# Query projection, range check and bias rows moved among the later spare jobs of a one-core attention kernel, and 29 instead of 30 key tiles on VectorE

## The chip, the core and the metric

One core of one Trainium2 chip runs the whole computation. Its engines work side by side and each takes its own instructions in order: TensorE (PE, matmuls into PSUM; PEld are its weight loads), VectorE (DVE), ScalarE (ACT), GpSimd (POOL), and SyncE (SP), which only issues DMAs here. The metric is the device time of one execution in microseconds (us).

## The reference, cut to what matters

Cross attention of 1024 queries over 6404 keys with 16 heads of width 8, followed by a feed-forward part with a main branch and two of eight experts, chosen once for all tokens.

```python
q = layernorm(x) @ Wq + bq;  k = ctx @ Wk + bk;  v = ctx @ Wv + bv      # 16 heads of 8
attn = softmax(clip(q @ k.T * 8 ** -0.5, -10000, 10000))                # nan: 1 / keys
x = x + (attn @ v) @ Wo + bo
main = gelu(h @ W1m + b1m) @ W2m + b2m                                  # h = layernorm(x)
x = x + a * main + (1 - a) * experts(h)                                 # a = clip(alpha, .1, 1)
```

The softmax is computed without a maximum when a bound on all scores shows that this is safe. That bound is what the code calls the check of ranges.

## The kernel before

**Passes, steps, tiles.** There are eight passes: four groups of four heads times two halves of 512 queries. In a pass each of 51 key tiles (50 of 128 keys, one tail of 4) is a step. A step has four chunks, one for each head, of 128 keys x 512 queries; the tail step has one chunk for all heads. Three chunks make a *tile* of 1536 columns in PSUM (`ps`, two of them), for which ScalarE runs one exponential (line 540) into one of four buffers. There are 496 tiles (`NT`), numbered through all passes. TensorE computes the scores of tile t+2 (line 1222), does what spare job stands at tile t, waits for exponential t and adds to the output the steps of values whose last chunk lies in tile t (line 1315). As four tiles hold three steps, every fourth tile has no step of values. TensorE is thus two tiles of scores ahead of ScalarE.

**Key tiles on VectorE.** `D_PLAN` takes 30 of the 400 full key tiles from ScalarE: VectorE computes their exponentials by a polynomial (lines 932 to 973, about 19 us of VectorE a key tile). A row of the plan is: pass, key tile, the tiles at which TensorE computes the four heads' scores into the spare bank, the order of the heads, and the tile at which the values are used. Such a score matmul runs beside those of the tile, on other rows of the array.

**Spare jobs.** `SPARE` lists what TensorE writes to the spare PSUM bank (`po[1]` in pass 0), by tile: V's projection in chunks (`V_AT`: chunk 2 at tile 2, then every third tile to chunk 12 at tile 32), the two halves of the range bound (`BOUND_TILES`, 3 and 7), the gather of their maxima (10), the rows (12: bo, alpha and the experts' first biases spread over the partitions), the scores for VectorE, and at a pass's end the tokens (line 1268). There is one bank: TensorE's `spare_job` (line 1232) waits until VectorE's `take_job` (line 737) has released the job before (`spare_taken`). Behind V's chunks 2 to 7, VectorE also splits K's segments 4 to 9 into two parts, which SyncE stores to DRAM and loads back in the layout of the scores.

**The head.** Ahead of the first scores TensorE transposes the context in 13 pieces and projects each to K (line 1097), ScalarE reads both. In between stand q replicated for group 0 (`qrep`, line 1131) and q itself (`qT`, line 1137, read by ScalarE in line 526). VectorE picks the two parts of group 0's q (`pick_q`, lines 680 to 682); its second half is picked behind bound 0. q itself serves the range check (`q_abs`, line 726) and groups 1 to 3: `split_q` (lines 672, 674, behind bound 1, tile 7) writes two parts, which GpSimd stores to DRAM (line 478) and loads back (line 382, twelve loads) and then fills V's tail buffer (lines 482, 485). VectorE waits for those fills before it copies V's tail in (line 897).

**The flag.** The gather's result is a flag (line 757). `NPRE` is 14: all engines run tiles 0 to 13, then wait for the flag and branch: the fast branch goes on with the tiles, the other computes everything in a general way. The inputs here take the fast branch.

**The epilogue.** `EPI_AT` puts steps of the first half's output projection, second layernorm and first feed-forward layer among the tiles of the last pass. Step 1 is the residual (line 776).

Of the kernel before, what the change touches and what calls it, by code (L numbers as in the profile page):

```python
# [33 lines left out]
BANK = 512  # L34
KCH = -(-NK // BANK)
NHALF = NQ // BANK
# [20 lines left out]
NPRE = 14  # L57
V_AT = {c: 3 * c - 4 for c in range(2, VCH)}
BOUND_TILES, GSUM_TILE, ROWS_TILE = (3, 7), 10, 12
# [59 lines left out]
]  # L119
DKT = [[kt for p, kt, *_ in D_PLAN if p == q] for q in range(NP)]  # L120

# [1373 lines left out]
```

## Time and profile before

| | |
|---|---|
| median of 3 runs | 776.45 us (776.31 to 778.46) |
| the profiled execution | 778.63 us, of which the span is 776.8 |
| PE busy | 729.8 us, 94% |
| ACT busy | 717.9 us, 92% |
| DVE busy | 618.7 us, 80% |
| POOL busy | 28.1 us, 4% |
| the exponentials, line 540 | 496 in 708.1 us |
| steps of values, line 1315, VectorE's and ScalarE's | 3200 matmuls |
| chain that ended last | PE 66%, ACT 17%, issue 14%, DVE 2%, DMA 1% |

Busy times are of one profiled execution. Matmuls are pipelined: several records overlap, so the time from one group's start to the next one's start is what a group costs, not its length. A row of the timeline gives the start, the length of a merged group, the engine, the line, what is written from what, how many instructions, and in brackets how long the engine was idle before it and what released it.

### The profile page before, as it was taken

Reading aid. Unit: us, or ns where it says so; the run is one execution under the profiler, and the core shown is the slowest. Engines: PE = TensorE matmul, PEld = TensorE weight load, DVE = VectorE, ACT = ScalarE, POOL = GpSimd, SP = SyncE. Lnnn points to the kernel's source line nnn. Section 1 sums busy time; section 2 is a strip of 40 time slices with the busy share of each in tenths; the row PEclk is TensorE's granted clock in tenths of the full one; section 3 lists DMA queues with packets and bytes.
Section 4 is the critical chain, followed back from the end, with each engine's and each line's share of the span. In section 5 each row is a group of like instructions: output and inputs, shape, how many; then the busy total and the mean of one; then the engine's idle time right before and its main releaser. Section 6 shows DMA issues by size and latency. Waiting matters only on the chain.

```text
span 776.8 us, 13354 instructions
## 1 busy us (share of the span) xinstructions
PE 729.8 (94%) x5398; PEld 218.1 (28%) x5398; DVE 618.7 (80%) x857; ACT 717.9 (92%) x575; POOL 28.1 (4%) x49
## 2 busy tenths in 40 slices
PE   5999999999999999999999999999999999999898
PEld 3534322222222222222222222222222223222457
DVE  6873369799969998799889998999889976986320
ACT  3788999999999999999999999999999999999751
POOL 5204000000000000000000000000000000000000
PEclk9899999999999999999999999999999999999999
DMA  5669100111110000111100000111100000000011
GB/s 166 179 196 258 42 1 2 35 35 35 35 35 1 2 1 1 37 41 43 42 10 2 1 1 18 35 35 40 47 1 1 1 1 1 2 0 2 1 54 30
DMA packets 18043, 28.53 MB, mean 37 GB/s; under 512 B 5286, under 2 KB 8732, under 8 KB 17980
## 3 DMA queue, kind: packets, MB, share of 16 engines
q1 hardware_dynamic: 12730, 23.71, 10.4%
q0 software_dynamic: 4032, 3.30, 1.8%
q8 instruction: 45, 0.74, 0.4%
q10 hardware_dynamic: 1218, 0.64, 0.3%
q14 instruction: 18, 0.15, 0.1%
HBM read 19.50 MB, written 8.13 MB: 36 GB/s over the span
## 4 chain that ended last, share of the span: by engine, by line
PE 66%; ACT 17%; issue 14%; DVE 2%; DMA 1%; SPq 0%; ACTq 0%
PE po L1315 34%; PE ps L1222 19%; ACT region_ctx L540 12%; ACT probs_own L540 4%; PE ps L1328 2%; PE po L1108 2%; PE po L1338 1%; PE ps L1097 1%; PE po L1301 1%; PE po L1222 1%; DVE pT L657 1%; DMA xres<-in_x 1%; PE po L1199 1%; PE ps L1085 1%; PE po L1169 0%
## 5 line engine op out<-in xcount | busy, mean ns | idle before, releaser
L540 ACT ACTIVATE region_ctx<-ps 128x1536 f32<-128x1536 f32 x372 | 523.0, 1493 | 9.8 <-PE ps L1222 8.6
L1315 PE MATMUL po<-region_ctx,v 128*9 128x512 f32 x2220 | 386.0, 595 | 0.3 <-ACT region_ctx L540 0.3
L1222 PE MATMUL ps<-qst,region_k 32*128 32x512 f32 x1480 | 249.1, 492 | 31.7 <-ACT region_ctx L540 22.5
L1222 PEld LDWEIGHTS ps<-qst,region_k 32*128 32x128 f32 x1480 | 95.7, 181 | 400.4 <-ACT region_ctx L540 279.7
L1315 PE MATMUL po<-probs_own,v 128*9 128x512 f32 x740 | 191.0, 595 | 0.0
L540 ACT ACTIVATE probs_own<-ps 128x1536 f32<-128x1536 f32 x124 | 185.1, 1493 | 2.3 <-PE ps L1222 2.2
L932 DVE TENSOR_SCALAR region_kT<-po 128x512 f32<-128x512 f32 x120 | 82.4, 687 | 44.0 <-PE po L1222 43.3
L935 DVE SCALAR_TENSOR_TENSOR region_kT<-region_kT,po 128x512 f32<-128x512 f32 x120 | 81.7, 681 | 0.3
L973 DVE SCALAR_TENSOR_TENSOR dres<-region_kT,dres 128x1024 f32<-128x1024 f32 x60 | 73.5, 1225 | 1.9
L970 DVE SCALAR_TENSOR_TENSOR dres<-region_kT,dres 128x1024 f32<-128x1024 f32 x60 | 73.2, 1220 | 0.2
L964 DVE SCALAR_TENSOR_TENSOR region_kT<-region_kT 128x1024 f32<-128x1024 f32 x60 | 73.1, 1219 | 0.0
L962 DVE SCALAR_TENSOR_TENSOR dres<-region_kT 128x1024 f32<-128x1024 f32 x60 | 73.1, 1218 | 0.0
L967 DVE SCALAR_TENSOR_TENSOR dres<-dres,region_kT 128x1024 f32<-128x1024 f32 x60 | 73.0, 1216 | 0.0
L1315 PEld LDWEIGHTS po<-region_ctx,v 128*9 128x9 f32 x2220 | 41.8, 88 | 66.7 <-issue 62.0
L1222 PE MATMUL po<-qst,region_k 32*128 32x512 f32 x120 | 55.4, 462 | 0.4 <-DVE xres L776 0.4
L953 DVE TENSOR_SCALAR region_kT<-region_kT 128x1024 uint32<-128x1024 uint32 x60 | 41.0, 684 | 0.0
L1315 PE MATMUL po<-dres,vd 128*9 128x512 f32 x240 | 31.4, 595 | 0.0
L697 DVE COPY v<-po 128x512 f32<-128x512 f32 (+1 forms) x13 | 8.8, 680 | 24.5 <-PE po L1108 24.5
L1315 PEld LDWEIGHTS po<-probs_own,v 128*9 128x9 f32 x740 | 19.5, 88 | 26.7 <-issue 25.6
L492 POOL TENSOR_TENSOR rstd<-rstd,powers 128x4 f32<-128x4 f32 x1 | 1.1, 1082 | 590.2 <-DVE rstd L629 590.2
L1222 PEld LDWEIGHTS po<-qst,region_k 32*128 32x128 f32 x120 | 21.8, 182 | 1.0 <-issue 1.0
L914 DVE COPY region_kT<-po 128x512 f32<-128x512 f32 x7 | 4.8, 692 | 17.0 <-PE po L1301 17.0
(219 smaller groups left out, 354.1 us busy)
## 6 DMA issues: line engine op xcount, KB each, us to landing
region_k<-k_dram SPq DMA_DIRECT2D x40, 320.0 KB, 3.3
k_dram<-kparts SPq DMA_DIRECT2D x18, 320.0 KB, 3.8
qst<-q_dram POOLq DMA_DIRECT2D x12, 128.0 KB, 9.6
region_ctx<-in_ctx SPq DMA_DIRECT2D x2, 624.0 KB, 9.0
q_dram<-dres POOLq DMA_DIRECT2D x2, 512.0 KB, 4.1
k_dram<-kparts SPq DMA_DIRECT2D x2, 322.0 KB, 8.4
region_ctx<-in_ctx SPq DMA_DIRECT2D x1, 576.0 KB, 7.4
xres<-in_x SPq DMA_DIRECT2D x1, 512.0 KB, 4.4
```

Source lines behind the costliest of these rows:

```text
L540: act.activation(probs_of(t)[:, 0:cols], ps[t % NSB][:, 0:cols], ACT.Exp, scale=ESCALE).then_inc(exp_ready, 1)
L932: d_count(("u", c), v.tensor_scalar(du[:, i % 2, part], src, MAGIC, None, ALU.add))
L935: v.scalar_tensor_tensor(df[:, i % 2, part], du[:, i % 2, part], MAGIC, src, ALU.subtract, ALU.subtract).then_inc(spare_taken, 1)
L953: d_count(("e", i), v.tensor_scalar(u.bitcast(U32), u.bitcast(U32), 23, None, ALU.logical_shift_left))
L962: d_count(("q1", i), v.scalar_tensor_tensor(res, f, A1, f, ALU.add, ALU.mult))
L964: d_count(("q2", i), v.scalar_tensor_tensor(q, f, A2, f, ALU.add, ALU.mult))
L967: d_count(("p1", i), v.scalar_tensor_tensor(res, res, B1, u, ALU.add, ALU.mult))
L970: d_count(("p2", i), v.scalar_tensor_tensor(res, q, B2, res, ALU.add, ALU.mult))
L973: v.scalar_tensor_tensor(res, f, R0, res, ALU.subtract, ALU.mult).then_inc(d_ready, 1)
L1108: last = mm(dst[:, (t % 4) * P:(t % 4 + 1) * P], lhsT, wv_sb[:, :], start=True, stop=True)
L1222: return mm(dst, kst[r, kt * P:(kt + 1) * P], qst[r, g, queries], start=True, stop=True)
L1315: last = mm(dst[QUAD * j:QUAD * j + V9, :], w, src, start=first, stop=last_one, skip_group_check=True)
```

## The change

q itself is no longer projected in the head. It becomes two spare jobs, at tiles 33 and 35, behind V's last chunk; VectorE instead of ScalarE reads it, and in the same job makes the absolute values for the bound. Behind its second half VectorE splits q and finishes the sum that the flag needs. The bounds move from tiles 3 and 7 to 37 and 39, the gather from 10 to 41, the rows from 12 to 44. The second half of the picked q moves from behind bound 0 to behind V's chunk 2. The branch moves from tile 14 to tile 47, so that all V chunks lie ahead of it; the keys' tail and the residual's bias are handled by VectorE behind the branch, the bias behind the wait for GpSimd's fills.

The plan of VectorE's key tiles has 29 rows. Pass 0 has none any more (it had one), pass 2 has five instead of four, pass 4 four instead of five, and all tiles are set anew; the first score job stands at 50 instead of 38. That makes 1492 chunks and 498 tiles, the last of one chunk. The epilogue's steps move too, and the tokens of pass 6 from tile 436 to 440.

```diff
-NPRE = 14
+NPRE = 47
 V_AT = {c: 3 * c - 4 for c in range(2, VCH)}
-BOUND_TILES, GSUM_TILE, ROWS_TILE = (3, 7), 10, 12
+Q_TILES, BOUND_TILES, GSUM_TILE, ROWS_TILE = (33, 35), (37, 39), 41, 44
 D_PLAN = [
-    (0, 49, (38, 40, 43, 45), (3, 1, 2, 0), 60),
-    (1, 49, (49, 52, 56, 59), (0, 1, 2, 3), 75),
-    (1, 48, (62, 71, 74, 76), (3, 1, 2, 0), 91),
+    (1, 49, (50, 52, 55, 57), (3, 1, 2, 0), 75),
+    (1, 48, (61, 64, 73, 75), (0, 1, 3, 2), 87),
...
-    (7, 47, (445, 448, 455, 458), (0, 1, 2, 3), 476),
-    (7, 46, (461, 466, 469, 475), (0, 3, 1, 2), 484),
+    (7, 47, (445, 447, 454, 456), (0, 2, 3, 1), 472),
+    (7, 46, (461, 467, 470, 473), (0, 2, 3, 1), 496),
 ]
-EPI_AT = [440, 444, 452, 464, 472, 480, 488]
+EPI_AT = [444, 452, 464, 476, 484, 488, 492]
...
-            act.wait_ge(bqs_ready, 1)
-            for n in range(NHALF):
-                act.wait_ge(q_psum, n + 1)
-                act.activation(qT[:, n * BANK:(n + 1) * BANK], po[n][:, :], ACT.Identity, bias=bqs[:, 0:1], scale=QSCALE,
-                               accum_out=ksum[:, KCH + n:KCH + n + 1]).then_inc(q_ready, 1)
...
-            link(v.scalar_tensor_tensor(q_abs, qT[:, :], -1.0, qT[:, :], ALU.mult, ALU.max))
...
                 if kind == "v":
                     take_v(i, src).then_inc(spare_taken, 1)
+                    if i == 2:
+                        pick_q(1)
+                elif kind == "q":
+                    cols = slice(i * BANK, (i + 1) * BANK)
+                    step(v.tensor_scalar(qT[:, cols], src[:, :], QSCALE, bqs[:, 0:1], ALU.mult, ALU.add))
+                    v.scalar_tensor_tensor(q_abs[:, cols], qT[:, cols], -1.0, qT[:, cols], ALU.mult, ALU.max).then_inc(spare_taken, 1)
+                    step(v.tensor_reduce(ksum[:, KCH + i:KCH + i + 1], qT[:, cols], AX.X, ALU.add))
+                    if i == NHALF - 1:
+                        split_q()
+                        step(v.tensor_reduce(kcol[:, 3:4], ksum[:, :], AX.X, ALU.add))
+                        step(v.tensor_tensor(kcol[:, 5:6], kcol[:, 3:4], bkc[:, :], ALU.add))
+                        v.tensor_scalar(kcol[:, 4:5], kcol[:, 5:6], 0.0, None, ALU.mult).then_inc(bounds_ready, 1)
                 elif kind == "bound":
                     v.tensor_reduce(gcol[:, i:i + 1], src[0:2 * H, :], AX.X, ALU.max).then_inc(spare_taken, 1)
-                    if i == 0:
-                        pick_q(1)
-                    else:
-                        split_q()
...
             with dve.If(safe != 0):
                 flink = chain(fast_step)
-                for n in range(JOBS_PRE, JOBS_V):
-                    take_job(n, flink)
-                    if SPARE[n][1:] == ("v", VCH - 4):
-                        add_bo(flink)
-                    if SPARE[n][1:] == ("v", VCH - 2):
-                        take_last_keys()
+                take_last_keys()
                 dve.wait_ge(spare_taken, JOBS_V)
                 dve.wait_ge(vones_ready, 2 + GH)
                 for j in range(GH):
                     r = slice(QUAD * j, QUAD * (j + 1))
                     v.tensor_copy(vtail[r, :, QUAD * j:QUAD * j + D],
                                   v9[r, FULL, :, 0:D].rearrange("p (g j) d -> p g j d", g=NG)[:, :, j, :]).then_inc(vtail_ready, 1)
+                add_bo(flink)
...
-            for n in range(NHALF):
-                pe.wait_ge(qrep_ready, n + 1)
-                mm(po[n][:, :], wq_sb[:, :], xnT[:, n * BANK:(n + 1) * BANK], start=True, stop=True).then_inc(q_psum, 1)
...
+                elif kind == "q":
+                    last = mm(po[1][:, :], wq_sb[:, :], xnT[:, i * BANK:(i + 1) * BANK], start=True, stop=True)
```

## Rows read from the trace of the kernel before

**Rows 1.** Busy by stretch: PE, PEld, DVE, ACT, POOL; clock, DMA share, GB/s.

```profile
24.50:37.00 12.50, 12.50 (x53) 6.66 (x52) 9.73 (x17) 10.97 (x31) 0.00 (x0) 1.00 0.54 157
98.00:600.00 502.00, 474.56 (x3664) 115.89 (x3660) 454.69 (x550) 498.14 (x368) 0.00 (x0) 1.00 0.08 21
```

**Rows 2.** Timeline of ACT: exponentials of tiles 0, 45 to 47, and 48.

```profile
37.05 1.45 ACT L540 ACTIVATE probs_own<-ps 128x1536 f32<-128x1536 f32 x1
...
106.21 4.21 ACT L540 ACTIVATE region_ctx<-ps 128x1536 f32<-128x1536 f32 x3
110.20 1.56 ACT L540 ACTIVATE probs_own<-ps 128x1536 f32<-128x1536 f32 x1
```

**Rows 3.** Chain that ended last, 20 to 45 us: start, length, what.

```profile
25.13 1.72 PE po L1137 x4
...
42.02 1.09 PE po L1108 x8
43.11 0.97 PE po L1315 x8
```

**Rows 4.** Exponentials by stretch: tiles 0-32, 50-65, passes 3, 4, 7; length, busy.

```profile
37.00:89.95 52.95, 46.44 (x33) 1.00 0.68 193
...
112.86:135.48 22.62, 21.82 (x17) 1.00 0.00 1
...
302.83:387.71 84.88, 84.08 (x63) 1.00 0.13 36
387.72:470.00 82.28, 81.57 (x61) 1.00 0.02 5
...
639.60:725.43 85.83, 84.17 (x62) 1.00 0.00 1
```

**Rows 5.** Timeline of PE: bound 0, gather, and rows, between the scores around them.

```profile
44.02 0.50 PE L1222 MATMUL ps<-qst,region_k 32*128 32x512 f32 x3
...
44.45 0.62 PE L1253 MATMUL po<-xn,bounds 128*32 128x512 f32 x1
...
46.28 0.73 PE L1222 MATMUL ps<-qst,region_k 32*128 32x512 f32 x6
...
56.04 0.21 PE L1257 MATMUL po<-ident,gcol 32*1 32x32 f32 x2
...
59.68 0.50 PE L1222 MATMUL ps<-qst,region_k 32*128 32x512 f32 x3
...
60.63 0.50 PE L1222 MATMUL ps<-qst,region_k 32*128 32x512 f32 x3
```

**Rows 6.** Timeline of DVE: absolute values, bound's maximum, and the split of q.

```profile
40.63 1.23 DVE L726 SCALAR_TENSOR_TENSOR xn<-qT 128x1024 f32<-128x1024 f32 x1
...
45.53 0.68 DVE L745 TENSOR_REDUCE gcol<-po 32x1 f32<-32x512 f32 x1 [0.43 <-PE po L1253]
...
52.54 0.67 DVE L672 CAST dres<-qT 128x1024 fp32r<-128x1024 f32 x1
...
53.25 1.23 DVE L674 TENSOR_TENSOR dres<-qT,dres 128x1024 fp32r<-128x1024 f32 x1
```

**Rows 7.** Timeline of DVE: its copy of V's last chunk (tile 32).

```profile
92.22 0.56 DVE L697 COPY v<-po 128x384 f32<-128x384 f32 x1 [3.73 <-PE po L1108]
```

**Rows 8.** Timeline of POOL's loads and fills, and of a copy beside a fill.

```profile
11.65 5.61 DVE L657 COPY pT<-ident 128x64 f32<-128x64 f32 x2
11.66 5.52 POOL L466 MEMSET region_ctxT<- 1x6432 f32 x1 [7.32 <-DVE xn L634]
...
59.96 6.99 POOL L382 DMA_DIRECT2D qst<-q_dram  x12 [4.30 <-DMA q_dram<-dres]
...
67.55 0.56 POOL L485 MEMSET vtail<- 4x4 f32 x4
```

**Rows 9.** Timeline: score job behind the residual, and the exponential it delayed.

```profile
657.07 0.47 PE L1222 MATMUL po<-qst,region_k 32*128 32x512 f32 x1 [0.45 <-DVE xres L776]
...
659.00 1.46 ACT L540 ACTIVATE probs_own<-ps 128x1536 f32<-128x1536 f32 x1 [0.78 <-PE ps L1222]
```

More of the change, by code:

```diff
@@ L153 @@
                + [(NORM_AT[p], "tokens", p) for p in range(NP - 1)] + [(t, "v", c) for c, t in V_AT.items()]
-               + [(t, "bound", n) for n, t in enumerate(BOUND_TILES)]
+               + [(t, "q", n) for n, t in enumerate(Q_TILES)] + [(t, "bound", n) for n, t in enumerate(BOUND_TILES)]
                + [(GSUM_TILE, "gsum", 0), (ROWS_TILE, "rows", 0)])
 JOBS_PRE = sum(t < NPRE for t, _, _ in SPARE)
-JOBS_V = SPARE.index((V_AT[VCH - 1], "v", VCH - 1)) + 1
+JOBS_V = JOBS_PRE
 SPLIT_BEHIND = {SPARE.index((V_AT[c], "v", c)): s for c, s in zip(range(2, VCH), range(4, NSEG))}
@@ L318, in build @@
         var_ready, std_ready, xn_ready = sem("var_ready"), sem("std_ready"), sem("xn_ready")
-        xnT_psum, xnT_ready, q_psum, q_ready = sem("xnT_psum"), sem("xnT_ready"), sem("q_psum"), sem("q_ready")
+        xnT_psum, xnT_ready = sem("xnT_psum"), sem("xnT_ready")
         ctxT_psum, ctxT_ready, tailT_ready = sem("ctxT_psum"), sem("ctxT_ready"), sem("tailT_ready")
@@ L669, in split_q @@
             def split_q():
-                dve.wait_ge(q_ready, NHALF)
                 v.tensor_copy(qparts[:, 0, :], qT[:, :]).then_inc(qparts_ready, 1)
@@ L724, in _ @@
             link(range_k(KCH - 1))
-            dve.wait_ge(q_ready, NHALF)
-            link(v.scalar_tensor_tensor(q_abs, qT[:, :], -1.0, qT[:, :], ALU.mult, ALU.max))
             link(v.tensor_reduce(kcol[:, 0:1], kmax[:, :], AX.X, ALU.max))
@@ L731, in _ @@
             v.tensor_scalar(bounds[:, H:2 * H], hmask[:, :], kcol[:, 2:3], ESCALE / SAFE_SCORE, ALU.mult, ALU.mult).then_inc(bounds_ready, 1)
-            link(v.tensor_reduce(kcol[:, 3:4], ksum[:, :], AX.X, ALU.add))
-            link(v.tensor_tensor(kcol[:, 5:6], kcol[:, 3:4], bkc[:, :], ALU.add))
-            v.tensor_scalar(kcol[:, 4:5], kcol[:, 5:6], 0.0, None, ALU.mult).then_inc(bounds_ready, 1)
             def take_job(n, step):
@@ L1010, in _ @@
                 glink(v.memset(gen[:, :], 0.0))
-                for n in range(JOBS_PRE, JOBS_V):
-                    take_job(n, glink)
                 dve.wait_ge(spare_taken, JOBS_V)
@@ L1373, in _ @@
             score_tile(0)
-            pe.wait_ge(q_ready, NHALF)
+            pe.wait_ge(qrep_ready, NHALF)
             project_v(0, po[0]).then_inc(v_psum, 1)
@@ L1422, in _ @@
                 pe.wait_ge(exp_ready, NPRE)
-                for n in range(JOBS_PRE, JOBS_V):
-                    spare_job(n)
                 with pe.Fori(0, H) as h:
```

50 rows, old and new, of the table D_PLAN are left out of this document.

## The prediction

> **What bounds the kernel now.** Three views were read in this order: the busy times by stretch, the chain of waits, and the starts of the exponentials (one per tile, so their starts are the clock of the loop).
>
> The stretches say that two engines share the bound. From 98 to 600 us ScalarE is busy 498.1 of 502.0 us and TensorE 474.6 [rows 1]. Undisturbed, three exponentials take 3.99 us (106.21 to 110.20), 1.33 a tile [rows 2]; a slower tile is one in which ScalarE waited for TensorE. From 24.5 to 37 us TensorE is busy all of 12.5 us [rows 1]: the work ahead of the first scores is TensorE's, and the chain runs through the q projection there [rows 3]. Tiles 0 to 32 take 52.95 us, not 33 x 1.33 = 43.9, and ScalarE is busy for only 46.4 of them [rows 4]: this stretch is TensorE's too.
>
> TensorE's slots, from start to start: the scores of a tile 0.43 us (44.02 to 44.45 [rows 5]), a step of values 0.97 to 0.98 [rows 3], three steps in four tiles. Four tiles are 4 x 0.43 + 3 x 0.98 = 4.66 us of TensorE against 5.32 of ScalarE: 0.17 us a tile is free for spare jobs. A V chunk every third tile (1.09 us [rows 3], 0.36 a tile) uses that up; behind tile 32 it is free again. That decides what a moved job costs.
>
> **The change, part by part.**
>
> *q out of the head.* Four matmuls, 1.72 us of the chain from 25.13 on [rows 3]. ScalarE's two reads of them go too, but behind them TensorE's chain runs on without a gap, so ScalarE's share is no second gain. First scores, and all behind them, 1.72 us earlier. If something hidden is late next (the stored first K segment, VectorE's maxima), the gain is 0. VectorE also loses the 1.23 us of the absolute values [rows 6] ahead of its second V chunk and gets the second half of the picked q behind that chunk; these offset each other, and the K segments that it splits there are wanted many tiles later. Term: -1.72, bounds -1.8 and 0.
>
> *Jobs out of tiles 3 to 12.* Each range bound lies between the scores at 44.02 and those at 46.28: 2.26 us, less 0.43 and 0.98 is 0.86 each [rows 5]. The gather's small matmuls take 0.16 to 0.21, the rows' matmuls 60.63 - 59.68 - 0.43 = 0.52 [rows 5]. The stretch is TensorE's, so all of it is won: 2 x 0.86 + 0.16 + 0.52 = 2.40. Term: -2.4, bounds -2.4 and -1.7 (ScalarE becomes the limit in places).
>
> *Jobs into tiles 33 to 44.* Counted on the old time axis from 92.11, where scores 35 start, a tenth ahead of VectorE's copy of V's last chunk at 92.22 [rows 7]: twelve scores of 0.434 (5.2), nine steps (8.8), q 2 x 0.86, bounds 2 x 0.86, gather 0.16 (3.6 together), and a wait of about 0.3, since the q job comes one tile behind V's last chunk, whose copy ends at 92.78 while TensorE is there at 92.54. Scores 46 end at 92.11 + 17.9 = 110.0, and exponential 46 starts at 110.1 instead of 107.54 (one tile behind 106.21 [rows 2]). The rows' job at 44 falls where slack is back: 0. Term: +2.55. Bounds: 0 (all beneath ScalarE's 1.33) and +4.5 (VectorE late by a microsecond at two of the jobs). I take the slot count, since it is the count that gives the time of tiles 0 to 32.
>
> The new waits on VectorE: q's first half must be read and made absolute before the second may overwrite the bank, 0.69 us (as the maximum over as many columns, 0.68) + 0.65 (half of 1.23, rounded up [rows 6]), and two tiles lie between: enough. Behind the second half stand on VectorE a sum (0.68), the split (0.67 + 1.23 [rows 6]) and three small steps (0.6), and only then the maximum of bound 0 (0.68 [rows 6]), for which TensorE's bound 1 waits: from 97.6, 0.69 + 0.65 + 0.68 + 1.90 + 0.6 + 0.68 = 5.2, so 102.8. TensorE gets there at about 102.9: a tie.
>
> *The flag and its branch.* They move from tile 14 to 47. At tile 14 TensorE goes from rows to the next scores at 60.63 without a pause [rows 5], so I give the branch 0 at both places (bounds 0 and +0.5). SyncE's next work behind the flag is group 1's K, 40 us later: nothing.
>
> *GpSimd's queue.* The split feeds two stores to DRAM, twelve loads, and then the fills of V's tail on GpSimd. From the end of VectorE's subtraction (53.25 + 1.23 = 54.48 [rows 6]) to the last fill (67.55 + 0.56 = 68.11 [rows 8]) it is 13.6 us. VectorE waits for these fills behind the flag, and behind that wait now stand the residual's bias (2.2 us) and then the first polynomial job (tile 50). On the old axis the subtraction ends at 101.6, the fills at 115.2, tail copies and bias at 118.2, and the first job's bank is free at 119.6; TensorE wants it for the next job (tile 52) at about 120.2. Term: 0, with 0.6 us to spare. The loads themselves are wanted in pass 2, 100 us later.
>
> Here the Trainium skill speaks against the change. The row first: a 128x64 copy on VectorE lasted 5.61 us [rows 8], as long as the GpSimd fill that began with it (5.52). The Trainium skill, "SBUF — State Buffer", section "Who interferes with whom", says that the two engines share a port pair which one instruction locks whole, and that GpSimd's writing of DMA descriptors is shut out while VectorE runs a copy of the two-port kind. By that rule the chain could grow by what copies lie beside it: the split's own two operations beside the first store, up to 1.9 us, to 15.5; the sum would stay, and the chance of the second rival would be 0.10. In the old place V's copies and K's splits stood beside the twelve loads, in the new one only a few short ones; no row of this trace shows a load held up, so the sum and the chances go by 13.6 us.
>
> *29 key tiles instead of 30 on VectorE.* ScalarE gets four more chunks: 1492 instead of 1488, thus one full tile more, +1.33, and a last tile of one chunk. In front of it TensorE has a step of VectorE's values (tile 496): 0.98 bare at the end, where such a filled slot cost 0.3 in the loop (4 x 0.43 + 4 x 0.98 = 5.64 us of TensorE for four tiles instead of ScalarE's 5.32); the short exponential hides under it. +0.7, bounds 0 and +1.0. VectorE's 19 us for that key are saved where it isn't the limit: 0.
>
> *Where the keys and the epilogue's steps now stand.* Pass 0 has no VectorE key. Its last 16 tiles took 22.62 us [rows 4], 1.33 above 16 x 1.33, as that key's step (tile 60) and two steps of one tile met; without it I take half: -0.7 (bounds -1.3 and 0). Pass 2 gets the fifth key and pass 4 gives it up. A pass of 62 tiles and four keys is 84.88 - 82.5 = 2.4 above ScalarE's count, the one of 60 tiles and five keys 82.28 - 79.9 = 2.4 [rows 4]: no difference; +0.3 for denser spots (bounds 0 and +0.7). In the last pass, the score job one tile behind the residual waited for VectorE's residual (0.45 us of TensorE's idle at 657.07) and cost ScalarE 0.78 [rows 9]; now it stands two tiles behind: -0.8 (bounds -1.0 and 0).
>
> **The sum.** -1.72 - 2.40 + 2.55 + 1.33 + 0.7 - 0.7 + 0.3 - 0.8 = -0.74. The profiled execution took 778.63 us (span 776.8, 1.8 around it); it would take 777.9. The median of the runs shown is 776.45, 2.2 below the profiled one, so the forecast is 776.45 - 0.74 = **775.7**. Single runs differ by as much as 2.2 us, more than the whole sum. What a measurement of this kernel can tell from no change is about 0.3%, or 2.3 us: faster means below 774.1, slower above 778.8.
>
> **The rivals.**
>
> *More is won.* If the moved jobs cost 1.7 instead of 2.55 as ScalarE's two tiles of lead bridge them, the last 0.98 is hidden, and the stall behind V's tail at the start of the last pass (85.83 us for 61 tiles, 4.6 above the count [rows 4]) gives back 0.9 with tokens now five tiles behind it: -0.74 - 0.85 - 0.7 - 0.9 = -3.2, 773.3. For it: the last pass has twice the excess of others. Against: its structure is the same. Chance 0.18.
>
> *Slower: GpSimd's chain holds VectorE at the fills.* Beyond 0.6 us TensorE stands at tile 52's job, and beyond another 2.7 (two tiles of scores in hand) ScalarE stands too: the rival decides from a chain of about 17 us, and each microsecond above costs one. A store's landing of twice the 4.3 us [rows 8] and loads at 0.9 instead of 0.58 us give 13.6 + 4.3 + 3.8 = 21.7: +4.4, 780.1. Against: DMA is nearly idle at that time, busier in the old place. Chance 0.08.
>
> *VectorE's serial work among the q and bound jobs.* The tie above becomes a wait: 0.7 us at bound 0, bound 1 and the gather each, nothing regained: +2.1, 777.8. Within 0.3%. Chance 0.12.
>
> *The head does not shrink*, something else being due at 36.4 us: 775.7 + 1.7 = 777.4. Chance 0.04.
>
> **How the numbers follow.** Forecast 0.58, its own range 774.0 to 777.6; the rivals 0.18, 0.08, 0.12 and 0.04. The range for 8 in 10 reaches into the first two: 773.2 to 779.2. Faster by over 0.3%: the first rival and a little of the forecast's edge, 0.20. Slower: GpSimd's chain and VectorE's waits together with a median drawn from the upper of the readings shown, 0.11. Within: 0.69.
>
> **What would show each step.** The first exponential at 35.3 instead of 37.05 us [rows 2]. Exponential 33 at 37.05 + 52.9 - 4.1 = 85.8. Exponential 46 at 107.5 - 4.1 + 2.55 = 106.0, with q and bound jobs back to back in TensorE's chain; VectorE releasing bound 1 would show the third rival. GpSimd's last fill some 13.6 us behind the subtraction, and TensorE not idle at tile 52. 498 exponentials, the last short. The last at 724 - 0.7. The prediction is wrong if the passes 1 to 6 differ by over 0.7 us from those of before, since I took them over as they are. What would also upset it is another drop of TensorE's clock, which these rows show at 1.00 from 24.5 us on [rows 1].

## The result

The changed kernel takes 778.13 us (median of 22 runs), the kernel before 776.45 (22 runs beside them): ratio 1.0025, 95% interval 1.0019 to 1.0031. It is slower by 1.7 us. That lies inside the 0.3% within which the prediction said "same", and inside its range, but the forecast was 0.7 us faster: the sign and 2.4 us are wrong.

The page of the kernel after, its span and busy times; they answer the table of the kernel before:

```profile
span 776.5 us, 13335 instructions
## 1 busy us (share of the span) xinstructions
PE 729.0 (94%) x5398; PEld 217.6 (28%) x5398; DVE 603.8 (78%) x841; ACT 717.5 (92%) x573; POOL 27.8 (4%) x49
```

VectorE works 15 us less (603.8 against 618.7), TensorE and ScalarE as much as before. None of the three says where the time went.

One thing has to be cleared first. The execution of the kernel before from which the rows ahead of the prediction come had lost time in its head: TensorE's granted clock fell to half between 16.8 and 23.6 us. The kernel before, run again, did not lose it. The same stretch in both, first the execution on which the prediction rests, then the second one (busy time of each engine with counts, granted clock, DMA share, GB/s):

```profile
16.80:23.60 6.80, 6.29 (x12) 3.12 (x13) 6.48 (x17) 1.97 (x4) 6.76 (x12) 0.50 0.47 93
```

```profile
16.80:23.60 6.80, 5.82 (x22) 2.90 (x21) 6.60 (x17) 3.77 (x8) 6.76 (x12) 1.00 0.48 93
```

Its first exponential starts at 34.84 instead of 37.05 us [rows 2], its span is 774.6 instead of 776.8, and its time 776.42 lies on the median. So the 2.2 us between the profiled execution and the median, which the prediction noted and subtracted without a reason, are this, and all comparisons below are with the second execution, named "before again".

The exponentials by stretch (length of the stretch, ScalarE's busy time with the count, granted clock, DMA share, GB/s) answer [rows 4]. The stretches begin at the starts of exponentials 0, 33, 50, of the first of pass 1, and so on. Before again:

```profile
34.78:87.70 52.92, 46.42 (x33) 1.00 0.66 194
87.70:110.60 22.90, 22.90 (x18) 1.00 0.00 1
110.60:133.24 22.64, 21.84 (x17) 1.00 0.01 1
133.24:217.59 84.35, 84.01 (x63) 1.00 0.14 40
217.59:300.54 82.95, 82.90 (x62) 1.00 0.01 1
300.54:385.45 84.91, 84.09 (x63) 1.00 0.13 36
385.45:467.83 82.38, 81.64 (x61) 1.00 0.02 5
467.83:552.54 84.71, 84.04 (x63) 1.00 0.13 36
552.54:637.39 84.85, 84.26 (x63) 1.00 0.02 5
637.39:721.76 84.37, 82.72 (x61) 1.00 0.01 1
```

After:

```profile
33.08:84.32 51.24, 46.34 (x33) 1.00 0.52 156
84.32:110.64 26.32, 23.19 (x18) 1.00 0.36 94
110.64:133.81 23.17, 23.04 (x18) 1.00 0.03 9
133.81:218.72 84.91, 84.05 (x63) 1.00 0.13 36
218.72:300.38 81.66, 81.20 (x61) 1.00 0.02 5
300.38:385.98 85.60, 84.18 (x63) 1.00 0.13 36
385.98:471.42 85.44, 84.06 (x63) 1.00 0.02 5
471.42:554.21 82.79, 82.79 (x62) 1.00 0.14 37
554.21:638.62 84.41, 83.87 (x63) 1.00 0.02 5
638.62:724.38 85.76, 84.03 (x62) 1.00 0.00 1
```

(A count can be one above the tiles of its stretch, where the exponential before it still ends inside.) From these two tables, with 1.33 us taken off where the kernel after has one tile more in the stretch:

| stretch | before again | after | difference, extra tiles taken off | predicted |
|---|---|---|---|---|
| up to the first exponential | 34.84 | 33.13 | -1.71 | -1.72 |
| tiles 0 to 32 | 52.92 | 51.24 | -1.68 | -2.40 |
| tiles 33 to 49 | 22.90 | 26.32 | +3.42 | +2.55 |
| rest of pass 0 (16 tiles, then 17) | 22.64 | 23.17 | -0.80 | -0.7 |
| passes 1 to 6 (369 tiles in both) and pass 7 up to its last exponential (60, then 61) | 588.52 | 590.57 | +0.72 | -0.5 |
| the extra tiles and what follows the last exponential | | | +1.88 | +2.03 |
| sum | | | +1.83 | -0.74 |

The last line but one: two more starts of exponentials are 2.66, and from the start of the last one to the end of the span it is 52.03 us instead of 52.81, since the last tile has one chunk only: 2.66 - 0.78 = 1.88. The sum agrees with the spans, 776.47 - 774.63 = 1.84. Three terms came out within 0.15 us (the extra tiles and the end for a wrong reason, see below), three did not: what was won early came to 0.7 less, the jobs put in cost 0.9 more, and the passes behind lost 0.7 where 0.5 was to be won.

### The profile page after: what moved, and what is told of

Same layout as the page of the kernel before. It is cut to its first block, busy times and chain, and to the rows that moved or that the text cites. A ratio compares the mean times of both kernels' runs of the same rounds, so it can differ in the third digit from the quotient of the medians.

```text
span 776.5 us, 13335 instructions
## 1 busy us (share of the span) xinstructions
PE 729.0 (94%) x5398; PEld 217.6 (28%) x5398; DVE 603.8 (78%) x841; ACT 717.5 (92%) x573; POOL 27.8 (4%) x49
## 4 chain that ended last, share of the span: by engine, by line
PE 63%; ACT 18%; issue 16%; DVE 2%; DMA 1%; ACTq 0%; SPq 0%
PE po L1303 32%; PE ps L1208 18%; ACT region_ctx L534 14%; ACT probs_own L534 4%; PE ps L1316 2%; PE po L1097 2%; PE po L1326 1%; PE po L1289 1%; PE ps L1086 1%; PE po L1208 1%; DVE pT L651 1%; DMA xres<-in_x 1%; PE po L1185 1%; PE po L1155 0%; PE ps L1326 0%
## 5 line engine op out<-in xcount | busy, mean ns | idle before, releaser
L534 ACT ACTIVATE region_ctx<-ps 128x1536 f32<-128x1536 f32 (+1 forms) x373 | 524.4, 1503 | 9.9 <-PE ps L1208 9.1
L534 ACT ACTIVATE probs_own<-ps 128x1536 f32<-128x1536 f32 x125 | 187.7, 1502 | 4.6 <-PE ps L1208 4.3
L923 DVE TENSOR_SCALAR region_kT<-po 128x512 f32<-128x512 f32 x116 | 79.5, 685 | 32.2 <-PE po L1208 31.5
L926 DVE SCALAR_TENSOR_TENSOR region_kT<-region_kT,po 128x512 f32<-128x512 f32 x116 | 78.8, 679 | 0.3
L964 DVE SCALAR_TENSOR_TENSOR dres<-region_kT,dres 128x1024 f32<-128x1024 f32 x58 | 71.0, 1225 | 1.8
L961 DVE SCALAR_TENSOR_TENSOR dres<-region_kT,dres 128x1024 f32<-128x1024 f32 x58 | 70.6, 1217 | 0.2
L953 DVE SCALAR_TENSOR_TENSOR dres<-region_kT 128x1024 f32<-128x1024 f32 x58 | 70.6, 1217 | 0.0
L955 DVE SCALAR_TENSOR_TENSOR region_kT<-region_kT 128x1024 f32<-128x1024 f32 x58 | 70.5, 1216 | 0.0
L958 DVE SCALAR_TENSOR_TENSOR dres<-dres,region_kT 128x1024 f32<-128x1024 f32 x58 | 70.4, 1213 | 0.0
L1208 PE MATMUL po<-qst,region_k 32*128 32x512 f32 x116 | 53.8, 464 | 0.4 <-DVE xnT L777 0.4
```

Of the source, the lines that this page charges most:

```text
L534: act.activation(probs_of(t)[:, 0:cols], ps[t % NSB][:, 0:cols], ACT.Exp, scale=ESCALE).then_inc(exp_ready, 1)
L923: d_count(("u", c), v.tensor_scalar(du[:, i % 2, part], src, MAGIC, None, ALU.add))
L926: v.scalar_tensor_tensor(df[:, i % 2, part], du[:, i % 2, part], MAGIC, src, ALU.subtract, ALU.subtract).then_inc(spare_taken, 1)
L953: d_count(("q1", i), v.scalar_tensor_tensor(res, f, A1, f, ALU.add, ALU.mult))
L955: d_count(("q2", i), v.scalar_tensor_tensor(q, f, A2, f, ALU.add, ALU.mult))
L958: d_count(("p1", i), v.scalar_tensor_tensor(res, res, B1, u, ALU.add, ALU.mult))
```

## Experiments

**Before again.** The kernel before, one execution. 

> The kernel before, unchanged, for a second trace. Theory: the profiled execution of before was 2.2 us above its median because TensorE's clock stood at 0.50 from about 17 to 23.6 us in the head (granted clock 0.996 over the span), which made the replicated-q matmuls 0.86 instead of 0.43 us each. Then a trace at clock 1.000 has its first exponential at about 34.9 us instead of 37.05, a span near 774.6, and loop intervals as before. Rival: the 2.2 us are spread over the loop, and the first exponential stays at 37.

Measured: 776.42 us, span 774.6, read above. It settles how much of the 2.2 us was the kernel's: none.

**plan29.** The kernel before with nothing changed but the table of VectorE's keys (29 rows) and the tiles of the epilogue's steps; q, the check and the rows stay where they were.

```diff
-    (0, 49, (38, 40, 43, 45), (3, 1, 2, 0), 60),
-    (1, 49, (49, 52, 56, 59), (0, 1, 2, 3), 75),
+    (1, 49, (50, 52, 55, 57), (3, 1, 2, 0), 75),
...
-EPI_AT = [440, 444, 452, 464, 472, 480, 488]
+EPI_AT = [444, 452, 464, 476, 484, 488, 492]
```

> The kernel before with the change's 29-row plan and epilogue tiles alone; q, bounds, gather and rows stay where they were. Theory from the two traces (one tile more 1.33, bare last step 0.57, pass 0's end -0.80, waits in passes 1 to 7 +0.76): +1.9, 778.3. By the terms of the prediction (1.33 + 0.7 - 0.7 + 0.3 - 0.8) +0.8, 777.3. If the plan were free and the moved jobs cost everything: 776.5.

Measured: 777.91 us (10 runs), ratio 1.0021 (1.0011 to 1.0030). The new table alone makes 1.5 of the 1.7 us. For the other half of the change, all the moved work, only 0.2 us are left, no more than single runs differ by: its gains (-1.71 - 1.68) and its price (+3.42) cancel. Exponential 50 starts at 110.6 us before again, in plan29 and in the kernel after alike.

**q_in_head.** The kernel after with q projected in the head again; only the check and the rows stay behind tile 33.

```diff
-Q_TILES, BOUND_TILES, GSUM_TILE, ROWS_TILE = (33, 35), (37, 39), 41, 44
+Q_TILES, BOUND_TILES, GSUM_TILE, ROWS_TILE = (), (37, 39), 41, 44
...
+            for n in range(NHALF):
+                pe.wait_ge(qrep_ready, n + 1)
+                mm(po[n][:, :], wq_sb[:, :], xnT[:, n * BANK:(n + 1) * BANK], start=True, stop=True).then_inc(q_psum, 1)
```

> The kernel after, but q is projected in the head again (matmuls, ScalarE's reads, absolute values and sum there) and the split stands behind bound 1; bounds, gather, rows, branch and plan as in after. Theory that each job costs what TensorE is late at its place: the head gives back 1.7, and the waits of ScalarE behind the q jobs (1.42 at tile 35 and most of 1.12 at tile 37) go: about -0.7 against after, 777.4. If moving q was worth its 1.72 less the 0.3 wait and the slots that ScalarE's slack can't hide, as the prediction had it, the two are within 0.3 of each other.

Measured: 783.24 us, ratio 1.0085 (1.0072 to 1.0099), far beyond what either theory allowed. The timelines of VectorE, TensorE and ScalarE in this run, a row of each (start, length, what, and in brackets the idle time before it and its releaser), then busy times and the granted clock behind them:

```profile
114.67 0.79 DVE L900 COPY vtail<-v 32x32 f32<-32x32 f32 x4 [5.68 <-POOL vtail L484]
```

```profile
119.18 0.47 PE L1224 MATMUL po<-qst,region_k 32*128 32x512 f32 x1 [3.11 <-DVE region_kT L939]
```

```profile
119.94 1.45 ACT L539 ACTIVATE region_ctx<-ps 128x1536 f32<-128x1536 f32 x1 [2.03 <-PE ps L1224]
```

```profile
120.60:124.10 3.50, 3.50 (x23) 0.74 (x23) 0.50 (x1) 2.24 (x2) 0.00 (x0) 0.53 0.02 5
```

Here the second rival of the prediction is seen at work. The split of q stood behind the second bound, GpSimd's stores landed late, VectorE stood 5.68 us at the last fill of V's tail, took the first score job only at 117.62, TensorE stood 3.11 us, ScalarE 2.03, and TensorE's clock was at 1.2 GHz for 3.5 us behind that. So the mechanism exists; the question is whether the kernel after pays any of it.

**empty.** The jobs at tiles that have no step of values beside them.

```diff
-Q_TILES, BOUND_TILES, GSUM_TILE, ROWS_TILE = (33, 35), (37, 39), 41, 44
+Q_TILES, BOUND_TILES, GSUM_TILE, ROWS_TILE = (33, 36), (40, 44), 46, 48
-NPRE = 47
+NPRE = 50
```

> The kernel after with the jobs at tiles that have no step of values (q at 33 and 36, bounds at 40 and 44, gather 46, rows 48, branch at 50). Theory that the limit is taken over a few tiles, not over the stretch (TensorE can be ahead by two tiles only): four tiles with one such job are 4.66 + 0.86 to 1.03 = 5.5 to 5.7 us against ScalarE's 5.32, so the jobs cost about 1.4 together instead of 3.43: -2.0 against after, 776.1. If the sum of slots over the stretch decides: no change, 778.1. If VectorE's serial work decides, part of it: 777.

Measured: 781.54 us, ratio 1.0056 (1.0042 to 1.0070). By exponential 50 it was ahead of the kernel after by 0.8 us (76.8 us from the first exponential instead of 77.6), less than half of the 2.0 that the first theory had, since the wait of 1.4 behind the first q job (tile 33) stayed; then it lost 4.6 more than the kernel after up to pass 1. Rows of VectorE, TensorE, and the stretch behind:

```profile
114.28 1.70 DVE L821 TENSOR_TENSOR xres<-xres,bob 128x128 f32<-128x128 f32 x8
```

```profile
117.57 0.76 PE L1208 MATMUL po<-qst,region_k 32*128 32x512 f32 x1 [2.48 <-DVE region_kT L926]
```

```profile
117.30:124.10 6.80, 6.53 (x31) 1.46 (x35) 1.66 (x4) 3.09 (x3) 0.00 (x0) 0.51 0.01 2
```

TensorE stood 2.48 us for VectorE, and then ran 6.8 us at half clock. VectorE was late not by the fills this time but by its own work between the rows' job (tile 48) and the first score job (tile 50): branch, copies, weights and residual's bias. One of the five executions kept a mean clock of 1.000 and took 779.06 us, the other four took 780.5 to 782.1.

**after_free and empty_free.** The kernel after, and empty, with VectorE freed: the bias is added in the rows' job, and the copies of V's tail stand behind the fourth score job.

```diff
+                    add_bo(step)
...
-                dve.wait_ge(vones_ready, 2 + GH)
+                dve.wait_ge(qparts_stored, 16 * PARTS)
...
-                add_bo(flink)
...
+                        if SPARE[n][2] == GH - 1:
+                            take_tail()
```

> The kernel after, with VectorE freed from GpSimd's chain: the residual's bias is added inside the rows' job at tile 44, and the copies of V's tail stand behind VectorE's fourth score job instead of ahead of the first, so that VectorE no longer waits for the last fill before it takes the first score job. Theory A (in the kernel after the chain has some 1 us to spare, so the order costs nothing): 778.1 in an undisturbed execution, within 0.5 us of the kernel after, and ScalarE's time from the first to the 50th exponential unchanged within 0.3 us. Theory B (the chain holds the loop already, the slower-side rival of the prediction): 776.0 to 777.0.

Measured: 778.09 us (11 runs), the kernel after has 778.13. Freeing VectorE brings nothing, so the kernel after pays nothing for GpSimd's chain. The trace of the kernel after says the same: GpSimd's last fill ends at 108.42, the bias at 111.44, and VectorE is then idle 1.65 us until there is a score job to take. Rows of POOL and DVE:

```profile
100.21 7.01 POOL L381 DMA_DIRECT2D qst<-q_dram  x12 [2.89 <-DMA q_dram<-dres]
...
107.81 0.61 POOL L484 MEMSET vtail<- 4x4 f32 x4
```

```profile
109.74 1.70 DVE L821 TENSOR_TENSOR xres<-xres,bob 128x128 f32<-128x128 f32 x8
113.09 0.69 DVE L923 TENSOR_SCALAR region_kT<-po 128x512 f32<-128x512 f32 x1 [1.65 <-PE po L1208]
```

> The run empty (q at tiles 33 and 36, bounds at 40 and 44, gather 46, rows 48) with the same freeing of VectorE. Theory A (empty lost its 3 us because VectorE was held by the last fill and the bias, TensorE then stood idle, and its clock fell behind that): no idle time of TensorE over 1 us between tiles 50 and 60, no fall of the granted clock there, and 0.7 below the kernel after: 777.4 (776.9 to 778.0). Theory B (the jobs themselves, or the writing out of q, cost it whatever VectorE does): 780 to 781.5.

Measured: 779.33 us (778.09 to 781.09, 6 runs); the profiled execution took 778.23. The half clock is gone from it, and with it 3.9 us against the profiled execution of empty (782.14), yet 0.87 is still lost at tile 54, for the reason seen in empty: with the bias in the rows' job at tile 48, that work ends at 113.47, the last keys' copies at 115.34, and TensorE stands 1.67 us. Both theories missed: VectorE's lateness is the cause, but my edit did not remove all of it. Four of the six executions had a granted clock of 0.995 to 0.998 on average and took 779.2 to 781.1.

**rows_first.** empty_free with the rows' job, and the bias in it, at tile 38.

```diff
-Q_TILES, BOUND_TILES, GSUM_TILE, ROWS_TILE = (33, 36), (40, 44), 46, 48
+Q_TILES, BOUND_TILES, GSUM_TILE, ROWS_TILE = (33, 36), (40, 44), 46, 38
```

> The run empty_free with the rows' job at tile 38 instead of 48, so that the 4 us of VectorE's work behind it (weights' scaling and residual) is over long before the first score job. Theory A (TensorE's idle time of 1.67 us at 116.9 us in empty_free, and the 0.87 of ScalarE behind it, came from VectorE's serial work between the rows' job and the first score job, and the slower runs of empty_free from the clock behind that idle time): 777.4 (777.1 to 777.7), no idle time of TensorE over 1 us between 110 and 125 us, and no run above 778.5. Theory B (the gain ahead of tile 50 is taken back in any case, because the chain on GpSimd sets when the first scores can be taken): 778.0 to 778.3.

Measured: 777.68 us, 777.53 to 778.15 in 11 runs, none of them with a clock below 0.999. TensorE no longer waits for VectorE between 112 and 124 us. So VectorE's work behind the rows' job was what was late, and the spread of empty_free went with it. Of the 0.7 us to be won against the kernel after, 0.45 arrive: the rows' job at tile 38 makes the scores of tile 41 late, exponential 41 starts 0.69 us late, and exponential 50 starts 77.3 us behind the first instead of 76.8.

**q_in_head_free.** q_in_head with VectorE freed in the same way.

> The run q_in_head (q projected ahead of the first scores, the check of ranges at tiles 37 to 41) with VectorE freed of GpSimd's chain as in after_free. It measures what moving q alone is worth when no chain holds the loop. Theory A (q costs in the loop what its slots and the wait for VectorE take there, 3.4 less the 2.1 that the three jobs alone cost in q_in_head, against 1.72 saved ahead of it): 0.3 to 0.5 above after_free, 778.4 to 778.6, no fall of the granted clock near 120 us. Theory B (the 5 us of q_in_head were no matter of VectorE's wait): 781 or more.

Measured: 778.51 us (6 runs), against 778.09 of after_free, which differs from it by q's place and what hangs on it (who reads q, and where the split stands). Of the 5.1 us that q_in_head lost, 4.7 were VectorE held by the fills and the clock behind it. q's move alone is worth 0.4 us. The single runs of the two overlap, but the traces agree: exponential 50 starts at 111.24 us here and at 110.66 in after_free.

**values.** Two steps of VectorE's values, which in the kernel after stand in the free tile ahead of the last steps of passes 2 and 3 (186 ahead of 187 and 188, 249 ahead of 250), are put earlier.

```diff
-    (2, 47, (162, 165, 169, 172), (1, 2, 0, 3), 186),
+    (2, 47, (162, 165, 169, 172), (1, 2, 0, 3), 184),
...
-    (3, 46, (224, 227, 231, 234), (2, 3, 0, 1), 249),
+    (3, 46, (224, 227, 231, 234), (2, 3, 0, 1), 245),
```

> The kernel after with two values steps of VectorE's rows put at tiles 184 and 245 instead of 186 and 249, where they stand right ahead of the last-chunk steps of their passes. Theory A (the longer waits of ScalarE at tiles 190 and 252, 1.05 each against 0.46 and 0.43 in the kernel before, come from these steps): 777.0 (776.8 to 777.4). Theory B (they come with the place of the last chunk in its tile): no change, 778.1 +- 0.3.

Measured: 777.69 us (11 runs), 0.44 below the kernel after, less than half of what theory A had. The starts of the exponentials show one move that paid and one that did not. With the step at 249 the exponentials of tiles 249 to 252 came 1.62 us late in sum, with it at 245 only 1.24. With the other at 184 the wait of 1.05 at tile 190 fell to 0.43, but 0.76 came up at tile 186 in its place.

**endvalue and values_last.** The last row's step of values, at tile 496 in the kernel after, is put at 484, and in the second run at 480, there with the step at 249 moved to 245.

```diff
-    (7, 46, (461, 467, 470, 473), (0, 2, 3, 1), 496),
+    (7, 46, (461, 467, 470, 473), (0, 2, 3, 1), 484),
```

> The kernel after with the last row's values step at tile 484 instead of 496. Theory A (at 496 that step runs bare behind the last exponential, which the prediction priced at 0.7): 777.5 (777.3 to 777.8). Theory B (the step costs TensorE the same wherever it stands): 778.1 +- 0.2.

Measured: 778.93 us, slower than the kernel after by 0.8: ScalarE waited 0.77 at tile 486, and the last exponential starts 0.93 later. The end did not get shorter by it. From the last exponential's start it is 51.78 us here and 52.03 in the kernel after, but also 51.78 in values and 51.81 in plan29, where the step stands at 496. Counted from there, TensorE is through with its values 0.85 us earlier, and then waits for ScalarE, whose activation is the same distance behind the last exponential in both. The activation in the kernel after, and the matmul that needs it, in endvalue:

```profile
726.34 1.91 ACT L539 ACTIVATE region_kT<-region_ctxT 128x2048 f32<-128x2048 f32 x1
```

```profile
729.23 0.71 PE L1155 MATMUL po<-w2m_sb,region_kT 128*128 128x128 f32 x4 [0.76 <-ACT region_kT L539]
```

The kernel after has this matmul at 728.31, 3.9 us behind the last exponential (724.43), endvalue 3.9 behind its own (725.36). So theory A was wrong in its premise: at 496 the step costs nothing at the end.

> The kernel after with two values steps of VectorE's rows moved: the one at 249 to 245 (0.67 of waits went with it in the run values), the last from 496 to 480, a tile without a step of the epilogue. Theory A (in endvalue the step met the epilogue's step at tile 484, and the wait of 0.77 at 486 is from that; at 480 only its own 0.3 to 0.5 is due): 777.0 (776.7 to 777.3), 1.1 below the kernel after. Theory B (TensorE pays a values step of 0.8 wherever it stands in the last pass): 777.5 to 777.9.

Measured: 782.04 us; every one of its 5 executions had a mean clock of 0.998 or less, and the profiled one had lost 2.3 us in its head to the half clock, as [rows 2] had. What belongs to the edit is seen in the rows of TensorE and ScalarE around tile 480:

```profile
707.71 1.05 PE L1303 MATMUL po<-dres,vd 128*9 128x512 f32 x8 [2.18 <-DVE dres L964]
```

```profile
709.23 1.45 ACT L534 ACTIVATE region_ctx<-ps 128x1536 f32<-128x1536 f32 x1 [2.20 <-PE ps L1208]
```

The last row's polynomial is not done at tile 480: TensorE stood 2.18 us for it, and ScalarE 2.20. Both theories priced only TensorE's slot. With scores up to tile 473, VectorE needs until about tile 482 for that row, so this step cannot be much earlier than 484. At 484, beside a step of the epilogue, it costs 0.8 (endvalue), at 496 nothing.

**best.** rows_first and values_last together. 

> rows_first and values_last together: jobs at 33, 36, 38, 40, 44 and 46, VectorE freed of the chain, and the two values steps moved. If the gains add: 778.1 less 0.7 less 1.1, 776.3 (775.9 to 776.9), level with the kernel before (776.4).

Measured: 781.59 us. The same wait at tile 480, and here the clock fell behind it; the row of TensorE and the stretch:

```profile
705.27 1.89 PE L1308 MATMUL po<-dres,vd 128*9 128x512 f32 x8 [2.19 <-DVE dres L968]
```

```profile
705.20:708.60 3.40, 3.33 (x19) 0.57 (x19) 0.59 (x1) 0.66 (x1) 0.00 (x0) 0.54 0.00 0
```

**joined.** rows_first with the step at 249 moved to 245 and the last step left at 496. 

> rows_first with the values step at 249 moved to 245, without the move of the last step that made TensorE wait for VectorE's last row in values_last. Theory A (the two parts are independent: rows_first measured 0.45 below the kernel after, and the waits at tiles 249 to 252 fall from 1.62 to 1.23): 777.3 (777.1 to 777.5). Theory B (a wait saved in pass 4 is taken back behind it): 777.7. Either way the kernel before, 776.4, stays ahead, by the extra tile and the last row's step.

Measured: 777.32 us (11 runs), ratio 1.0012 (1.0003 to 1.0021). The two gains add, 0.45 and 0.36. The rows of ScalarE at the start of pass 4, in the kernel after and in joined, show the second of them:

```profile
389.81 4.20 ACT L534 ACTIVATE region_ctx<-ps 128x1536 f32<-128x1536 f32 x3 [0.93 <-PE ps L1208]
```

```profile
389.16 4.21 ACT L534 ACTIVATE region_ctx<-ps 128x1536 f32<-128x1536 f32 x3 [0.31 <-PE ps L1213]
```

It is the fastest of the kernels with 29 keys, and the kernel before, 776.34 in the runs beside it, still leads by 1.0 us. No run here beats the kernel before.

## Why the prediction was wrong

*The head: right.* 33.13 instead of 34.84; both q matmul pairs were TensorE's, and nothing else was due. The forecast of 35.3 stood on the disturbed axis; the difference is what counts.

*Jobs out of tiles 3 to 12: mechanism right, size 0.72 too large.* The prediction took the stretch as TensorE's alone and gave all 2.40. Its lower bound, "ScalarE becomes the limit in places", is what happened: 1.68. Without the jobs ScalarE follows at once at several of these tiles, and what TensorE then saves cannot move an exponential. Measured from start to start with 1.33 taken off, the waits behind tiles 5, 9 and 16 before again were 0.93, 0.93 and 0.85; after, 5 and 9 are gone, 16 is 0.55, and one of 0.54 has come up at tile 7.

*Jobs into tiles 33 to 41: the count of slots was right, its end point wrong.* TensorE's rows of the kernel after, from the scores of tile 35 on:

```profile
86.52 0.50 PE L1208 MATMUL ps<-qst,region_k 32*128 32x512 f32 x3
87.34 1.10 PE L1238 MATMUL po<-xnT,wq_sb 128*128 128x512 f32 x2 [0.31 <-DVE v L690]
88.36 0.61 PE L1303 MATMUL po<-probs_own,v 128*9 128x512 f32 x3
...
91.18 1.12 PE L1238 MATMUL po<-xnT,wq_sb 128*128 128x512 f32 x2
92.24 1.05 PE L1303 MATMUL po<-region_ctx,v 128*9 128x512 f32 x8
...
97.64 0.62 PE L1241 MATMUL po<-xn,bounds 128*32 128x512 f32 x1
...
99.48 0.74 PE L1208 MATMUL ps<-qst,region_k 32*128 32x512 f32 x6
```

The wait of 0.3 for VectorE's copy is there as predicted (0.31). From scores 35 to scores 42 it is 99.48 - 86.52 = 12.96 us. The prediction's prices give 7 x 0.434 + 6 x 0.98 + 1.72 + 1.72 + 0.3 = 12.66. The difference of 0.30 lies in q's slots, 1.02 and 1.06 (87.34 to 88.36, 91.18 to 92.24) instead of 0.86 each; the other slots came to 0.06 less. But the prediction counted on to tile 46. It let the scores of tile 46 end 17.93 (its sum, rounded to 17.9 there) less 12.66, 5.27 us, behind the start of scores 42, and the exponential start 0.1 later. ScalarE can't do that: exponential 42 starts when its scores are done, 0.55 behind their start (100.03 - 99.48), and four tiles of ScalarE are 5.32, together 5.87 instead of 5.37. The slack of TensorE behind the last large job was set against the cost of the jobs, 0.50 us of it, and ScalarE cannot use slack that comes after it was late. The rows of ScalarE show where it was:

```profile
89.89 1.45 ACT L534 ACTIVATE probs_own<-ps 128x1536 f32<-128x1536 f32 x1 [1.32 <-PE ps L1208]
...
93.77 2.79 ACT L534 ACTIVATE region_ctx<-ps 128x1536 f32<-128x1536 f32 x2 [1.02 <-PE ps L1208]
...
100.03 1.45 ACT L534 ACTIVATE region_ctx<-ps 128x1536 f32<-128x1536 f32 x1 [0.79 <-PE ps L1208]
```

1.32, 1.02 and 0.79 us, and no wait afterwards. The loss is fixed at tile 42; 0.50 for the end point and 0.30 for the slots are 0.80 of the 0.87 that were missing. This also corrects "ScalarE's two tiles of lead": when TensorE stood 3.11 us in q_in_head, ScalarE stood 2.03, so the lead was 1.1 us, and at tile 480 of values_last 2.18 became 2.20, so there it was none.

*VectorE among the q and bound jobs (third rival): no.* The tie held. VectorE's maximum of bound 0 ends at 97.52 (96.85 + 0.67), and TensorE's bound 1 began at 97.64, without a wait for it:

```profile
96.85 0.67 DVE L744 TENSOR_REDUCE gcol<-po 32x1 f32<-32x512 f32 x1
```

*GpSimd's chain (second rival): not in this kernel.* From the end of the subtraction at 96.48 (95.25 + 1.23) to the last fill at 108.42 it is 11.9 us, less than the 13.6 taken over, mostly as GpSimd waited 2.89 instead of 4.30 us [rows 8] for the stores to land. after_free shows that it costs nothing. But the price given to the rival, one microsecond for each above 17, was too low: in q_in_head the fall of the clock came on top. (Its example was also summed too low: a chain of 21.7 us is 4.8 beyond 16.9, not 4.4.)

The rule on the shared port that was weighed there (the Trainium skill, "SBUF — State Buffer", "Who interferes with whom") would have made the chain longer by up to 1.9 us, for the split's two operations. By that section only the cast is of the two-port kind, the subtraction is not, and the rows agree: the first store's issue lasted 0.57 us in the kernel after with the subtraction beside it. The rule itself is seen in the old place, in before again, where VectorE casts K for its own split, from SBUF to SBUF, while GpSimd issues. Rows of POOL and DVE:

```profile
52.57 0.88 POOL L478 DMA_DIRECT2D q_dram<-dres  x1 [0.69 <-DVE dres L674]
52.86 0.47 DVE L691 CAST kparts<-region_kT 128x640 fp32r<-128x640 f32 x1
```

The same issue takes 0.54 us in the kernel after, without such a cast. Of the twelve loads in before again two took 0.84 and 0.86 us, each beside such a cast, the others 0.60 to 0.65, and the twelve 7.44 us instead of the 7.01 in the kernel after. In the execution of [rows 8] they took 6.99, and only the second store's issue was held (0.88). So the new place, with none of these casts, took 0.3 to 0.8 us out of the chain, the other way round than the prediction had weighed it.

*29 keys: the sum was right, half of it by luck.* The extra tile is 1.33, and what came on top is 0.55 instead of 0.7. But the prediction put that on TensorE's step of values at tile 496, bare at the end, with the short exponential hidden under it. It is the reverse: the step hides behind ScalarE's activation (endvalue), and the 0.55 is ScalarE's, 1.33 for one more start less the 0.78 by which the end is shorter, as the last exponential takes 0.60 instead of 1.45. The first rival had the step hidden; that the exponential would count in its place, neither had. The short exponential and the step, ACT and PE of the kernel after:

```profile
724.43 0.60 ACT L534 ACTIVATE region_ctx<-ps 128x512 f32<-128x512 f32 x1
```

```profile
725.19 1.04 PE L1303 MATMUL po<-dres,vd 128*9 128x512 f32 x8
```

*The passes: this step failed.* -0.8 for the epilogue's stall and +0.3 for denser spots were -0.5; measured is +0.72. The residual's own stall is gone: in the kernel after it stands at tile 452 with the next score job at 454, and TensorE does not wait there. But the new table puts the epilogue's first step (tile 444) one tile ahead of a score job (445), as the second had been, and TensorE waits there for VectorE's copy, in the row of the kernel after:

```profile
654.67 0.46 PE L1208 MATMUL po<-qst,region_k 32*128 32x512 f32 x1 [0.45 <-DVE xnT L777]
```

ScalarE stood 0.41 for it instead of 0.78 [rows 9], a gain of 0.37; and ScalarE's wait behind V's tail, at the start of the last pass, grew by as much, from 0.80 to 1.17. So the -0.8 became 0. Pass by pass, from the windows with 1.33 for each tile: pass 1 +0.56, pass 2 +0.04, pass 3 +0.69, pass 4 +0.40, pass 5 -0.59, pass 6 -0.44. The prediction compared how many keys a pass has, but not how near its steps of values stand to the last-chunk step. plan29, where the moved jobs play no part, has the same excess in every pass within 0.06 us; so it is the table. For pass 4 the run joined shows the cause: the step at 249 stood too near to the last-chunk step. For the start of pass 3 the cause is open; the one move tried only shifted the wait. The +0.56 of pass 1 was not tested; its rows have one new wait above 0.2 us, of 0.81 ahead of exponential 128, beside the last step of the pass. The gains of passes 5 and 6 were not tested either.

*The sum.* -0.74, plus 0.72 (early tiles), plus 0.87 (jobs), minus 0.10 (pass 0), plus 1.22 (passes), minus 0.15 (end), is +1.82: the measured 1.83. The prediction named its own test, passes 1 to 6 within 0.7 us, and in sum that held (+0.66), yet only as gains in 5 and 6 stood against losses in 1, 3 and 4.

## What to carry to other kernels

Where one engine feeds another tile by tile, count the lateness of moved jobs up to the last job, and give nothing back for the slack behind it. Work moved from ahead of a TensorE-bound loop into it is mostly paid again there (of q's 1.7 us, 0.4 were left), and what the room for it takes from another engine's share (here a key tile of VectorE, 1.5 us with its new table) can be the real price: ask for that first. When a table is set anew, look at every pair of a step and the next job on the same bank again, not only at the pair that stalled before. A step that looks bare at the end costs something only if its engine is the one that is waited for there. A profiled execution that lies off the median should be explained by its clock row before its rows are used as an axis.

## What the runs showed of the hardware

*A pause of TensorE in the busy loop can cost more than itself.* Behind 3.11, 2.48 and 2.19 us without work (q_in_head, empty, best) the granted clock was near 0.5 (0.53, 0.51 and 0.54, which is 1.2 GHz) for 3.5, 6.8 and 3.4 us, and a step of values took 1.89 us instead of 1.05. Behind the 2.18 us at tile 480 in the profiled execution of values_last and the 1.67 us of empty_free it stayed at 1.00, 2.4 GHz, though other executions of empty_free have a lower mean clock and take up to 2.9 us more. So pauses of about 2 us cost in some executions and not in others. A low mean clock alone does not prove such a pause: the kernel after has none there, and 3 of its 22 executions still took 779.7 to 783.2 us at a mean clock of 0.995 to 0.998; no trace shows where they lost it. The Trainium skill, "TensorE: Matmul & The Clock Gate", Part 1, says that the gate follows how busy the engine was recently and has these two levels alone; in these rows the falls stand behind pauses, and the stretches lie at 1.00 or near 0.5.

*The landing of q's stores to DRAM varies.* Behind the second issue GpSimd waited 2.9, 4.7 and 5.1 us for it in three kernels that differ in where the jobs stand (after, q_in_head, empty), and 4.3 and 3.6 us in two executions of the same kernel, the one before. That makes GpSimd's chain 11.9 to 14.0 us. A margin of a microsecond on such a chain is none.

*q's two fp32 matmuls over 128 columns of weights took 1.02 and 1.06 us as a job*, the bound's over 32 columns 0.86 (99.48 - 97.64 - 0.98), among the same neighbours, while in the head four in a row took 1.72 [rows 3].
